# Attention plus mixture of experts on one core: the slots that no row takes are written by seven indirect stores of a row tile instead of three large stores of zeros, and early experts' splits and VectorE's late order move

## The reference, cut to what matters

```python
x = hidden_states                                  # (2, 1024, 512) float32
xn = layernorm(x)
q, k, v = split(xn @ w_qkv.T + b_qkv)              # one head of 512
s = softmax(q @ k.T / sqrt(512)) @ v @ w_out.T + b_out
logits = xn @ router_w + router_b                  # 8 experts
top-2 of logits, full_w = softmax of the two       # per row
h = silu(xn @ expert_w[e] + expert_b[e])           # for the two chosen e
ffn = (sum of full_w * h) @ proj_w + proj_b
y = xn + ffn
g = silu(norm_w * y / sqrt(mean(y * y) + 1e-6))
out = x + s * g
```

## Time and profile before

| what | value |
|---|---|
| median of 3 runs | 486.03 us |
| the profiled execution, its own time | 488.05 us |
| its span, first to last instruction | 486.3 us |
| outside the span | 1.75 us |
| mean granted TensorE clock | 0.991 of full speed |
| moved by DMA | 115.77 MB, 238 GB/s over the span |

### The profile page before, as it was taken

The page is one execution under the profiler, slowest core; times in us unless marked ns, Lnnn a source line. Parts: engine busy times, 40 slices in busy tenths (PEclk is TensorE's granted clock), DMA queues, the critical chain, the costliest instruction groups (busy, mean ns, idle before and its releaser), DMA issues.

```text
span 486.3 us, 7100 instructions
## 1 busy us (share of the span) xinstructions
PE 471.4 (97%) x2116; PEld 385.6 (79%) x2117; DVE 324.0 (67%) x479; ACT 214.9 (44%) x311; POOL 233.6 (48%) x333
## 2 busy tenths in 40 slices
PE   9999979987999999999999999999999999999995
PEld 7878756866788888888888888888888888888884
DVE  4875954729743335988988888762597764857762
ACT  3694733224231154744644444422655441644550
POOL 5688335260677866700300000744567874377234
PEclk9999999989999999999999999999999999999999
DMA  8958999976798499779789665897455865445512
GB/s 314 351 202 304 279 348 372 411 230 194 247 328 301 187 308 303 240 230 276 221 262 280 196 199 191 300 311 276 131 181 165 258 193 176 143 144 171 174 42 88
DMA packets 81390, 115.77 MB, mean 238 GB/s; under 512 B 6784, under 2 KB 40592, under 8 KB 81360
## 3 DMA queue, kind: packets, MB, share of 16 engines
q1 hardware_dynamic: 68272, 79.72, 52.0%
q0 software_dynamic: 6896, 23.36, 13.9%
q10 hardware_dynamic: 6192, 12.32, 7.0%
HBM read 66.09 MB, written 49.28 MB: 237 GB/s over the span
## 4 chain that ended last, share of the span: by engine, by line
PE 86%; DVE 5%; DMA 3%; ACT 2%; issue 2%; ACTq 1%; SPq 0%; DVEq 0%
PE ab L1771 21%; PE ab L1772 20%; PE ab L1773 20%; PE sc L1773 6%; PE sc L1771 6%; PE sc L1772 6%; PE tp L1777 2%; DMA xs<-p_scratch 2%; DMA p_scratch<-prob 2%; ACTq L422 1%; PE sc L1874 1%; PE sc L1833 1%; PE tp L1863 1%; DVE small L1526 1%; ACT t_h L994 1%
## 5 line engine op out<-in xcount | busy, mean ns | idle before, releaser
L892 POOL DMA_INDIRECT y<-y_scratch,pos x32 | 33.5, 1047 | 78.4 <-DMA y_scratch<-yt_so 63.6
L1771 PE MATMUL ab<-W,st_h 128*128 x156 | 60.7, 389 | 0.0
L1772 PE MATMUL ab<-W,st_h 128*128 x156 | 60.7, 389 | 0.0
L1773 PE MATMUL ab<-W,st_l 128*128 x156 | 60.7, 389 | 0.0
L1771 PE MATMUL sc<-xt_h,t_h 128*128 128x512 f32 x128 | 51.0, 398 | 2.2 <-ACT xn L1116 2.2
L1773 PE MATMUL sc<-xt_h,t_l 128*128 128x512 f32 x128 | 50.5, 394 | 0.0
L1772 PE MATMUL sc<-xt_l,t_h 128*128 128x512 f32 x128 | 50.4, 394 | 0.0
L877 POOL DMA_INDIRECT rows_scratch<-xb,pos x32 | 31.5, 985 | 23.1 <-DVEq L1446 14.1
L1155 ACT CAST st_h<-tp 128x512 fp32r<-128x512 f32 x39 | 22.9, 587 | 42.5 <-PE ab L1773 41.5
L1526 DVE TENSOR_REDUCE small<-sc 128x1 f32<-128x1024 f32 x16 | 19.5, 1221 | 22.1 <-PE sc L1773 21.8
L1771 PEld LDWEIGHTS ab<-W,st_h 128*128 128x128 f32 x156 | 29.3, 188 | 6.1
(11 more groups left out here) (300 smaller groups left out, 1240.3 us busy)
## 6 DMA issues: line engine op xcount, KB each, us to landing
rows_scratch<-xn ACTq DMA_DIRECT2D x3, 3328.0 KB, 22.2
xb<-in_expert_w POOLq DMA_DIRECT2D x6, 1024.0 KB, 9.6
...
```

The lines of the kernel that those rows point to most:

```text
L892: pool.indirect_dma_start(y[:, q, :], None, y_d, bass.IndirectOffsetOnAxis(pos[:, GB * s + p:GB * s + p + 1], 0))\
L1771: nc.tensor.matmul(dst, lh, rh, start=start, stop=False)
L1772: nc.tensor.matmul(dst, lh, rl, start=False, stop=False)
L1773: return nc.tensor.matmul(dst, ll, rh, start=False, stop=stop)
```

## The change

- `clear_slots`, its three stores and the two waits for them go. So does the tile of zeros.
- `EMPTY` = 7. After the positions VectorE works out, in 11 small instructions, the 7 x 128 slots that no row takes (`pos0`): for the n-th empty slot, n plus the rows of all experts whose gap begins at or before n. `routed` is then counted to 2. The computation of `texp` follows in the same part of `choose()`, so that this last part has 14 instructions and stands ahead of `t_lo(0, 1, 2)` and `t_lo(0, 1, 3)` instead of behind them.
- GpSimd, after the 32 scatters, stores the finite tile `sbias` to those slots with seven indirect stores (`filled`). SyncE waits for all seven before it loads the first pair.
- VectorE: `t_lo(0, 1, 0)` goes behind `pt_low(0)` and `row_max(3)`, and the positions go ahead of `t_lo(0, 1, 1)`.
- ScalarE: `early_high(0)` goes ahead of `exp_0(0)`, and `early_high(1)` behind `pt_split(0)`.
- GpSimd: only `early_low(0, c)` stands ahead of the scatter; `early_low(1, c)` is put between the scatters of tiles 4 to 7 of the order.
- TensorE waits for 8 of the 16 early low parts before slot tile 0, and for all 16 before slot tile 1.

VectorE before, behind the part of `choose()` that ends with the first slot tiles (line 1436): `t_lo(0, 1, 0)` is the first 1339, `pt_low(0)` is 1544, `row_max(3)` is 1526 to 1529, `t_lo(0, 1, 1)` the second 1339.

```diff
 
     SLOT_TILES = 2 * T // P + E - 1
     LAST = SLOT_TILES - 1
+    EMPTY = SLOT_TILES - 2 * T // P
 
 
     EARLY = (2, 0, E - 1, 1)
...
+        nth = sb("nth", [P, EMPTY])
+        pos0 = sb("pos0", [P, EMPTY], I32)
...
-        zeros = xn[:, 0:1, :]
...
-        zero_set = sem("zero_set")
-        zero_in = sem("zero_in")
+        filled = sem("filled")
...
                 return bt_h[:, :, w], bt_l[:, :, w]
             return wk_h[:, :, w], wk_l[:, :, w]
 
-        def clear_slots(eng, n):
-
-            w = slice(n * SLOT_TILES // 3, (n + 1) * SLOT_TILES // 3)
-            eng.dma_start(rows_t[:, w, :], zeros.to_broadcast([P, w.stop - w.start, D])).then_inc(zero_in, 16)
-
         def in_groups(v):
 
             return v.rearrange("p (n q) -> p n q", n=KC)
...
             load_raw(sp, 4)
             for g in range(GB):
                 sp.wait_ge(sent[g], 64)
+            sp.wait_ge(filled, 16 * EMPTY)
             load_pair(0, 0)
 
             sp.wait_ge(ptr_done, GB - 1 - QB)
...
                       allow_small_or_imprecise_dtypes=True).then_inc(const, 1)
             pool.iota(slot_i[:, :, :], [[1, SLOT_TILES], [0, E]], base=0, channel_multiplier=0,
                       allow_small_or_imprecise_dtypes=True).then_inc(const, 1)
-            pool.memset(zeros, 0.0).then_inc(zero_set, 1)
+            link(pool.iota(nth[:, :], [[P, EMPTY]], base=0, channel_multiplier=1,
+                           allow_small_or_imprecise_dtypes=True))
             link(pool.memset(rw[:, :, :], 0.0))
             link(pool.memset(rb_bc[:, :], 0.0))
 
...
                     load_raw(pool, BY_BUFFER[k + 2])
 
 
-            for k in range(2):
-                for c in range(KC):
-                    early_low(k, c)
-            pool.wait_ge(zero_in, 48)
+            for c in range(KC):
+                early_low(0, c)
             pool.wait_ge(routed, 1)
             for n in range(G):
                 g = (n + GB) % G
...
                 for pos in (pos1, pos2):
                     pool.indirect_dma_start(slots_d, bass.IndirectOffsetOnAxis(pos[:, g:g + 1], 0),
                                             sent_rows[:, g % GB, :], None).then_inc(sent[g % GB], 16)
-                if n >= 3 * KC:
+                if KC <= n < 2 * KC:
+                    early_low(1, n % KC)
+                elif n >= 3 * KC:
                     early_low(2, n % KC)
+            pool.wait_ge(routed, 2)
+            for n in range(EMPTY):
+                pool.indirect_dma_start(slots_d, bass.IndirectOffsetOnAxis(pos0[:, n:n + 1], 0), sbias[:, :], None)\
+                    .then_inc(filled, 16)
             for c in range(KC):
                 early_low(3, c)
             for m in range(2 * len(LATER)):
...
                 if 1 <= t < 5:
                     qk_high(t - 1)
                 v_hi(0, t)
-                if t == GB - 4:
-                    act.wait_ge(zero_set, 1)
-                    clear_slots(act, 0)
             act.wait_ge(ln_done, 3)
             for g in range(GB, GB + 4):
                 normalise(g)
...
             fold_high(KC + 3)
             act.wait_ge(rt_done, 1)
             nc.scalar.copy(lt[0], sc[0:2 * NP, 0, :, :].rearrange("p a n -> p (a n)")).then_inc(lt_out, 1)
-            clear_slots(act, 1)
-            clear_slots(act, 2)
             act.wait_ge(qk_split, 6)
             hi(GB)
             hi(GB + 1)
...
                 nc.scalar.activation(out, whole, ACT.Exp, bias=small[:, 4 + j % QB, 1:2], scale=SCALE,
                                      accum_out=small[:, 4 + j % QB, 2:3]).then_inc(exp_done, 1)
 
+            early_high(0)
             exp_0(0)
-            early_high(0)
             act.wait_ge(gate_d, 1)
             nc.scalar.activation(small[:, 10, :], small[:, 9, :], ACT.Exp).then_inc(gate_e, 1)
 
-            act.wait_ge(zero_in, 48)
             exp_0(1)
+            pt_split(0)
             early_high(1)
-            pt_split(0)
             exp_0(2)
             t_hi(0, 1, 0)
             t_hi(0, 1, 1)
...
                 dve.sem_inc(routed, 1)
                 yield
 
+                before, gap = small[:, 1, 0:E], small[:, 9, 0:E]
+                link(vec.tensor_copy(starts[:, 0, E:2 * E], total))
+                src, back = 0, 1
+                while back < E:
+                    link(vec.tensor_tensor(starts[:, 1 - src, E:2 * E], starts[:, src, E:2 * E],
+                                           starts[:, src, E - back:2 * E - back], ALU.add))
+                    src, back = 1 - src, 2 * back
+                link(vec.tensor_tensor(before, starts[:, src, E:2 * E], total, ALU.subtract))
+                link(vec.scalar_tensor_tensor(gap, first, float(P), before, ALU.mult, ALU.subtract))
+                passed = wide(8).rearrange("p g e -> p (g e)")[:, 0:EMPTY * E].rearrange("p (n e) -> p n e", e=E)
+                link(vec.tensor_tensor(passed, nth[:, :].unsqueeze(2).to_broadcast([P, EMPTY, E]),
+                                       gap.unsqueeze(1).to_broadcast([P, EMPTY, E]), ALU.is_ge))
+                link(vec.tensor_tensor(passed, passed, total.unsqueeze(1).to_broadcast([P, EMPTY, E]), ALU.mult))
+                place = small[:, 1, 0:EMPTY]
+                link(vec.tensor_reduce(place, passed, AX.X, ALU.add))
+                link(vec.tensor_tensor(place, place, nth[:, :], ALU.add))
+                link(vec.tensor_copy(pos0[:, :], place))
+                dve.sem_inc(routed, 1)
+
                 link(vec.tensor_tensor(slot_i[:, :, :], slot_i[:, :, :],
                                        first.unsqueeze(1).to_broadcast([P, SLOT_TILES, E]), ALU.is_ge))
                 of_tile = wide(9).rearrange("p g e -> p (g e)")[:, 0:SLOT_TILES]
...
             next(routing)
             row_max(2)
             next(routing)
-            t_lo(0, 1, 0)
             pt_low(0)
             row_max(3)
+            t_lo(0, 1, 0)
+            next(routing)
             t_lo(0, 1, 1)
-            next(routing)
+            next(routing, None)
             t_lo(0, 1, 2)
             t_lo(0, 1, 3)
-            next(routing, None)
             p_turn(1)
             pt_low(1)
             attn_out(0)
...
             pe.wait_ge(assigned, 1)
             for i in range(PEEL):
                 if i == 0:
+                    pe.wait_ge(e_lo, KC * (EARLY.index(0) + 1))
+                elif i == 1:
                     pe.wait_ge(e_lo, KC * len(EARLY))
                 elif i < E and i in LATER:
                     pe.wait_ge(*lows_done(i))
```

## The result

The kernel after took 490.95 us (median; 489.36 to 492.54), the kernel before beside it 486.95 us (485.49 to 488.60). The ratio is 1.0086, with a 95% interval of 1.0065 to 1.0106: slower, by less than the 1% that I had called measurable, and 11 us above the forecast of 480.0, outside its range. So the two traces differ by only 1.3 us where the medians differ by 4.0.

The account below looks back on a forecast made before the run. TensorE was busy 97% of the span, so only its idle and slow stretches could be won. 488.05 us minus 6.5 at `attend_tile(0)` plus 0.5 for the fills gave 482.0, less 2.0 to the median: 480.0, range 476.5 to 485.5.

Parts of the forecast that it names:

- Part 1: Zero stores' issue goes: no TensorE wait near 70 us, second logit rows at 75.5 instead of 79.46, gain 4.0.
- Part 2: `early_low(0)` moves ahead of VectorE's choice of experts: TensorE's wait near 102 us and its slow clock, 3.75 us, go.
- Part 3: First probabilities' store and load back take 9.4 us instead of 16.7; transposes start at 98.4 (96.5 to 102).
- Part 4: VectorE's chain bounds: `attend_tile(0)` 19.0 us behind the transposes, at 117.4 instead of 123.86, gain 6.5 (3 to 8.4).
- the sum: Profiled execution 488.05 minus 6.5 plus 0.5 gives 482.0; its 2.0 above the median taken off: 480.0.
- Part 5: Last fill lands at 175.6, pair transposed from 180.4, slot tile 0 at 185 to 186: hidden, 0.5 us given.
- Rival A: Fills land late beside raw weights, each microsecond past 176.6 one less gain: 481.5 to 484.5, at 483; chance 0.24.
- Rival C: Fill wait ends the attention once the last fill lands after 183.1; slower, 490 us; chance 0.06.

Follow-up runs that it names:

- slots_behind: Kernel after, with the eleven position instructions and `texp` moved behind `t_lo(0, 1, 2)` and `t_lo(0, 1, 3)`: 491.02 us.
- undisturbed session: Later session in which the kernel before, run unchanged, took 487.23 us and the kernel after 491.28 us; its run of before is the undisturbed run.
- two_fills: Kernel after, but the first pair load waits for the first two fills only, the second pair load for the other five: 487.40 us.
- two_fills_raw_behind: Kernel after, with the first pair load waiting for two fills only and GpSimd's 1 MB raw load issued behind the fills: 489.76 us.
- late_fills_s_first: Kernel after: first pair waits for two fills; five fills, GpSimd's raw loads held until it landed; SyncE's second raw load behind it, `store_s(4)` earlier: 493.38 us.
- late_raw: Kernel after, but GpSimd's load of expert 6's raw weights waits until the first pair has landed: 489.23 us.
- sessions of the second kind: Sessions in which the unchanged kernel before takes about 503 us; in the first kind it takes about 487. The kernel after takes 491 to 492 in both.
- disturbed one: Kernel before, unchanged, profiled in a session where it is slow, with VectorE and ScalarE stopping until 155.5 us: 502.35 us.
- session 4: Session with both kernels unchanged, the kernel before at its slow time: before 502.35 us, after 491.78 us, ratio 0.978.

## Why the prediction was wrong

- **Part 1** held: second logit rows at 75.77 (75.5 forecast), no slow clock near 70.
- **Part 2** held: the low parts ended at 86.8, before VectorE's choice, and the wait near 102 went.
- **Part 3** held: `exp_0(0)` ended at 88.6 (88.8), the transposes of the first probabilities began at 99.25 (98.4).
- **Part 4** held in its number and, in part by luck, not in its mechanism: `attend_tile(0)` 19.0 us behind those transposes, as forecast, at 118.2 (117.4). VectorE's chain is the bound, but at `t_lo(0, 1, 0)`, which TensorE waits 3.3 us for at 110.45; the fourteen instructions, 3.8 of the 19.0 in the forecast, cost 0.5, as the run slots_behind shows. The slow matmuls behind that wait, which the forecast had at nothing, are part of what fills the time instead. None of the new instructions with two inputs in SBUF was held up beside the scatters. But its gain was counted against one execution: 123.86 was late for the kernel before, which in the undisturbed session had 122.04. The gain is 3.8 us against that execution and 5.6 against the first one, and not 6.5. It was a second mistake, in **the sum**, to take the 2.0 us by which the first execution was slow off the result too, when up to 1.8 of them (123.86 less 122.04) were in the 6.5 already.
- **Part 5** is the step that failed: "An indirect store lands in 2.7 to 6.1 us, 3.9 at the median: 175.6" and "The pair needs 4.2 to 5.3 us". The last fill landed at 179.3, and the pair needed 8.0. VectorE transposed 7.0 us later than I said (187.40 for 180.4): the last fill was issued 2.0 us late (173.68 for 171.7; the scatter began 0.3 late and took 1.6 longer), landed in 5.7 us and not 3.9 (1.8), and the pair took some 3.2 more. Landing and pair were priced from transfers that had had room. Fills and 3 MB of raw weights shared the engines at a share of 1.02, and the pair ran beside another 1 MB. The experiments bear this out. From the issue of the second fill to the pair load that waits for it were 9.2 us with 3 MB of raw weights issued ahead of the fills (two_fills), 7.8 with 2 MB (two_fills_raw_behind) and 5.2 with 1 MB and without the other five fills (late_fills_s_first); and the pair took 4.6 us where no raw load of GpSimd ran beside it (late_raw).
- **The miss in numbers.** For the profiled execution I had forecast 482.0, and it took 489.36. Of these 7.4 us, 5.0 are slot tile 0 (191.93 for 186.9), and 2.3 come behind it, mostly the half-clock stretch, for which the sum had no term. The other 3.6 of the 11 are the 2.0 counted twice and the 1.6 by which this execution lies under its median.
- **Rival A** named this course. By its own price, one less for each microsecond past 176.6, a landing at 179.3 leaves a gain of some 3 us; it had no term for a slow pair or a slow clock behind the wait. **Rival C** had the end: "the fill wait is the new end of the attention", but with a threshold of 183.1 for the last landing. At 179.3 it was not crossed, and still the kernel lost. I gave C 0.06, with late fills as its only term; fills and pair were both late, each beside large loads.
- **Unseen** altogether: the part of the change that pays. I had counted `early_low(1)` among the scatters as 4.8 us of GpSimd's time and nothing else. In sessions of the second kind it is the whole of a gain of 2.2%.

Open: what differs between the two kinds of session, and by what path GpSimd's row stops the other engines. An instruction supply that stalls would be one, but is not shown. For it: TensorE's gaps are "issue", and the profile counts one transfer of queue 8, of kind "instruction", from 138 to 156 us in the undisturbed run of before and none in the disturbed one. The count of the undisturbed run (transfers, MB, share):

```profile
q8 instruction: 1, 0.02, 0.7%
```

Against it: in the disturbed run this transfer comes between 159 and 160 us, some 4 us after VectorE and ScalarE had gone on, so it didn't end their stop and may only be late like all else. And in the kernel after of session 4 it came at 145 to 147 us, ahead of the stop that ended at 156.13.

The Trainium skill, "Runtime: NRT & Kernel Launch", section "Instruction fetch mechanics", calls the cost of crossing from one block of instructions to the next mostly hidden. If that is what the 18 us ahead of 155.46 are, it is not hidden here; no run shows that it is.
